# A recurrence of 2,048 steps on two engines: one product of the guarded norm issued behind the sum of squares

## The reference

```python
def step(h, inp):
    x_t, dt_t, B_t, C_t, xr_t = inp
    h_carrier = h.mean(axis=1)
    T = jnp.cos((c_phase(xr_t) - c_phase(h_carrier)) / 2.0) ** 2
    alpha = jnp.exp(dt_t[..., None] * A_neg)
    expo = 1.0 + (1.0 - alpha) * KAPPA * (1.0 - T[:, None, :])
    mag, ph = (c_mag(h), c_phase(h))
    cmag = jnp.minimum(jnp.exp(expo * jnp.log(mag + 1e-08)), 10.0)
    h = from_polar(cmag, ph)
    Bx = B_t[:, None, :, :] * (dt_t * x_t)[:, :, None, None]
    h = h + Bx
    h = from_polar(jnp.tanh(c_mag(h)), c_phase(h))
    y_t = jnp.einsum('bnc,bdnc->bd', C_t, h)
    return (h, y_t)
```

## Time and profile before

| | |
|---|---|
| median of 3 runs | 12692.01 us (12689.93 to 12693.14) |
| the profiled execution | 12694.92 us, span 12693.1 us |
| the recurrence's stretch in it | about 275 to 9440 us: 2,048 steps |
| busy in the whole span | PE 84%, DVE 80%, ACT 66%, PEld 42% |

### The profile page before, as it was taken

One profiled execution on the slowest core, in us unless ns is written; L12 is line 12 of the kernel. 1 busy time (PEld: TensorE's weight loads), 2 busy tenths in 40 slices (PEclk: granted clock), 3 DMA queues, 4 the chain that ended last, 5 costly groups with the idle time before them and its releaser, 6 DMA issues. The chain is left out here.

```text
span 12693.1 us, 256258 instructions
## 1 busy us (share of the span) xinstructions
PE 10620.3 (84%) x68398; PEld 5374.3 (42%) x68414; DVE 10121.4 (80%) x56587; ACT 8430.5 (66%) x42451; POOL 95.0 (1%) x165
## 2 busy tenths in 40 slices
PE   6888888888888888888888888888887978898998
PEld 5333333333333333333333333333344546653335
DVE  5888888888888888888888888888874948868875
ACT  6777777777777777777777777777764722264666
POOL 0000000000000000000000000000000100000000
PEclk8666667666666666666666666666678978998999
DMA  1000100001000100001000010001000000011100
GB/s 57 15 15 15 21 15 15 15 17 20 15 15 15 21 15 15 15 15 22 15 15 15 16 21 15 15 15 21 15 10 12 1 24 6 7 35 46 29 24 22
DMA packets 339618, 229.88 MB, mean 18 GB/s; under 512 B 27662, under 2 KB 324183, under 8 KB 337884
## 3 DMA queue, kind: packets, MB, share of 16 engines
q1 hardware_dynamic: 338140, 213.30, 7.9%
HBM read 187.41 MB, written 25.43 MB: 17 GB/s over the span
## 5 line engine op out<-in xcount | busy, mean ns | idle before, releaser
L548 PE MATMUL scan_p_car<-scan_warm 128*128 128x448 bf16 x15872 | 5455.5, 490 | 993.3 <-DVE scan_state_ps L674 985.4
L548 PEld LDWEIGHTS scan_p_car<-scan_warm 128*128 128x128 bf16 x15872 | 1513.7, 117 | 3681.5 <-DVE scan_state_ps L674 2094.0
L595 ACT ACTIVATE scan_act_ps<-scan_state_ps 128x64 f32<-128x64 f32 x2048 | 426.0, 208 | 1888.6 <-DVE scan_state_ps L674 1888.6
L595 ACT ACTIVATE scan_act_ps<-scan_act_ps 128x64 f32<-128x64 f32 (+1 forms) x8193 | 1611.6, 197 | 65.5
L536 PEld LDWEIGHTS scan_p_car<-scan_hs,scan_mean_mat 32*32 32x32 f32 x16392 | 372.2, 125 | 1846.5 <-DVE scan_hb L677 1834.2
L677 DVE SCALAR_TENSOR_TENSOR scan_uw<-scan_w,scan_rsq 128x64 f32<-128x64 f32 x2048 | 461.3, 225 | 854.2 <-ACT scan_rsq L595 854.2
L541 PE MATMUL scan_p_car<-scan_eps_row,ones 1*128 1x3 f32 x4102 | 1021.3, 316 | 39.1 <-DMA scan_a_log<-L_attn_a_A_log 38.9
L536 PE MATMUL scan_p_car<-scan_hs,scan_mean_mat 32*32 32x2 f32 x16392 | 548.5, 191 | 590.3 <-DVE scan_hb L677 568.0
L570 PE MATMUL scan_p_y<-scan_c_masked,scan_hb 128*64 128x4 f32 x16384 | 1037.8, 229 | 0.0
L674 DVE TENSOR_TENSOR scan_c<-scan_V,scan_power_ps 128x64 f32<-128x64 f32 x4096 | 724.6, 218 | 277.8 <-issue 47.6
L541 PEld LDWEIGHTS scan_p_car<-scan_eps_row,ones 1*128 1x128 f32 x4102 | 843.3, 255 | 72.0 <-DMA scan_a_log<-L_attn_a_A_log 39.3
(11 more groups left out here) (453 smaller groups left out, 18358.4 us busy)
## 6 DMA issues: line engine op xcount, KB each, us to landing
scan_step_in<-scan_scratch SPq DMA_DIRECT2D x520, 256.0 KB, 6.2
qk_scratch<-qkv_parts SPq DMA_DIRECT2D x32, 384.0 KB, 2.5
attn_qT<-qk_scratch SPq DMA_DIRECT2D x192, 64.0 KB, 2.2
attn_kT<-qk_scratch SPq DMA_DIRECT2D x192, 64.0 KB, 2.2
scan_scratch<-prep_dts SPq DMA_DIRECT2D x32, 256.0 KB, 2.1
x<-L_attn_a_x SPq DMA_DIRECT2D x1, 4096.0 KB
out<-x SPq DMA_DIRECT2D x1, 4096.0 KB
filter_in_taps<-c_kT SPq DMA_DIRECT2D x1, 2048.0 KB
```

The lines of the kernel that those rows point to most:

```text
L548: nc.tensor.matmul(p_car[slot][:, 64:512], warm[:, 0:P], warm[:, 64:512], start=True, stop=True)
L595: nc.scalar.activation(dst, src, func, **kw).then_inc(counts[par]["act"], 1)
```

## The change

The product `na` and the sum `r2` change places on VectorE. `na` no longer waits by itself for `sq0`, since `r2` in front of it has waited for `sq1`. The list `DVE_STEP` follows, so that the waits for `r2` (ScalarE's `l`, TensorE's matmuls) and for `na` (`n2`) count to the new places. No instruction is added or removed.

```diff
-DVE_STEP = ["c0", "c1", "w0", "w1", "sq0", "sq1", "na", "r2", "n2", "bx0", "bx1", "uw0", "uw1", "h0", "h1", "nh", "hp", "Vm", "dot", "dl", "s", "V"]
+DVE_STEP = ["c0", "c1", "w0", "w1", "sq0", "sq1", "r2", "na", "n2", "bx0", "bx1", "uw0", "uw1", "h0", "h1", "nh", "hp", "Vm", "dot", "dl", "s", "V"]
...
                                 tt(sem, sq[:, comp, :], w[:, comp, :], w[:, comp, :], ALU.mult)
-                            after(dve, "dve", "sq0", par, k)
-                            stt(sem, na[:, :], w[:, 0, :], 2 * EPS_PHASE, sq[:, 0, :], ALU.mult, ALU.add)
                             after(dve, "dve", "sq1", par, k)
                             tt(sem, r2[:, :], sq[:, 0, :], sq[:, 1, :], ALU.add)
+                            stt(sem, na[:, :], w[:, 0, :], 2 * EPS_PHASE, sq[:, 0, :], ALU.mult, ALU.add)
                             after(dve, "dve", "na", par, k)
                             tt(sem, n2[:, :], na[:, :], sq[:, 1, :], ALU.add)
```

## The result

The changed kernel took 12,744.3 us in the median of six executions, against 12,691.0 us for the kernel before in the same comparison: a ratio of 1.0038, 95% interval 1.0028 to 1.0049, so 36 to 62 us slower. One of the six was slow, 18,728.7 us at a mean granted clock of 0.555, and is left out of the ratio; the other five lie between 12,732.9 and 12,748.0 us. The forecast was 12,721 us and a slowdown. Its range (12,696 to 12,760) holds the measured time, which lies 1 us above the band of its main case (12,708 to 12,743); its 29 us are somewhat more than half of the 48 us that the ratio gives.

The account below looks back on a forecast made before the run. A dependency chain through `sq`, `r2`, `l`, `M`, `E`, `L1`, `R` bounds the kernel, no engine being full. 8 ns for late `ln2` plus 6 of extras, 14 ns a step, 29 us, gave a median of 12,721 us, range 12,696 to 12,760.

Parts of the forecast that it names:

- main case: Whole recurrence: 8 to 25 ns a step slower, 12,708 to 12,743 us; chance 0.60.
- `r2` starts at 388: VectorE, ns from the start of `sq0`: `r2` starts at 388 instead of 406, 18 earlier.
- the longer: Rival, own-result hand-over on VectorE of 52 ns: `r2` gains nothing, 44 ns a step lost, 12,782 us; chance 0.14.
- the shorter: Rival, own-result hand-over on VectorE below 30 ns: at 21 ns a gain of 18 ns a step, 12,655 us; chance 0.10.
- `na` takes the next slot, `n2` starts at 775: VectorE, ns from `sq0`: `na` starts at 523, ends at 741; `n2` starts at 775, 233 later than before.
- `ln2` is held by `n2`, `E` by `ln2`: ScalarE: `ln2` waits for `n2` until 1,035 instead of 1,027; `E`, queued behind it, also comes 8 ns later.
- The extras, 6 ns out of 0 to 17: Longer instructions from a standstill: 0 to 7 ns each for `r2` and `n2`, 0 to 3 for `ln2`; 6 taken.
- What is hidden: `bx0`, `bx1` move 0.24 us later inside VectorE's wait for `rsq`, 0.43 us in a plain step; TensorE's matmuls shift.
- The rule that the slots alone count: Rival from the Trainium skill, own-engine waits on VectorE cost nothing: 135 ns a step gained, 276 us, 12,416 us; chance 0.01.
- What the profile would show: Step time line: `r2` 0.39 and `n2` 0.78 behind `sq0`, `ln2` 0.03 behind `n2`; waits naming `n2`, a few tens of us.

## Why the prediction was right, and where its size was off

1. *`r2` starts at 388.* The time line has 0.38 to 0.39, the mean of the steps is 388, and the idle time in front of it is 34.1 ns, the hand-over that was taken from other layers. Right, and with it both rivals that hung on another hand-over, the longer and the shorter, are gone.
2. *`na` takes the next slot, `n2` starts at 775.* It starts 783 ns behind the first square on the mean, after another 34.1 ns of waiting. Right to 8 ns, and these belong to point 4.
3. *`ln2` is held by `n2`, `E` by `ln2`.* Right, and shown from four sides: free `n2` and the loss turns into a gain; one slot later costs nothing, two cost 44 ns; put `E` in front and it starts 0.24 behind `M`.
4. *The extras, 6 ns out of 0 to 17.* This is the term that was mis-sized. `na` follows `r2`, which starts from a standstill, by 142 ns and not by the slot of 135, so `n2` comes 7 ns later; and `n2` takes 233 ns and not 226, 7 more. `r2` takes 233 and not 227 as well, but `ln2` waits for `n2` and not for `M`, so this is hidden. The stretch agrees: 22.8 ns a step were measured where 8 were due without extras. So the extras are about 15 ns, near the upper end. The rows gave that end (`uw0` 225 against `na` 218) and I discounted it, because it was of another kind of instruction. 8 to 25 ns was the forecast's own range; 22.8 lies in it. Without extras the change would have cost 16 us, less than the 25 us that the prediction took for no change. So that the slowdown came out clear hung on the term that was put too small, and to that extent the call of "slower" was lucky; the mechanism was not.
5. *What is hidden.* `bx0`, `bx1` and the output product stayed hidden: VectorE still waits 0.21 us for `rsq`, as said. On TensorE the prediction gave no number, only that "the chain meets TensorE again only when `h1` is there". That holds for this change, which starts the three matmuls earlier: the mean starts 54 ns behind `h1` as before. But the cover is thin: the same matmuls 0.14 us later cost 65 us.
6. *The rule that the slots alone count.* By it the change would have gained 276 us. It is refuted for these instructions by the same 34.1 ns of idle time and by the measured slowdown.
7. *What the profile would show.* I had expected the waits to name `n2` as ScalarE's releaser. They don't: its group (which holds `lnh` too) has no idle time in front of it, because `M` is still running (6082.61 + 0.21) when `ln2` starts at 6082.77:

```profile
L595 ACT ACTIVATE scan_act_ps<-scan_norm_ps 128x64 f32<-128x64 f32 x4036 | 855.6, 212 | 0.0
```

An instruction that is late by less than the overlap leaves no trace in the waits. Only the distances from start to start show it.

## What to carry to other kernels

Where two short results leave one engine and the next engine takes them in a fixed order, what counts is which of the two has less to spare, not which the chain runs through today. Before moving a producer, compare its delay with its consumer's slack: here 241 ns of delay (233 predicted) and a sum that took 7 ns longer stood against 225 of slack, and a gain of 18 in front of them came to nothing. Put something independent between a short instruction and the one that reads it; where that can't be done, count, for instructions of this size, the hand-over (34 ns) and the standstill (7 ns) at each such place.

## What the runs showed of the hardware

- VectorE starts 128x64 instructions every 135 ns. One that reads the result of the one before starts 34 ns behind its end, for 128x64 as for 128x1536; for 128x64 that is 252 ns from start to start (`na` to `n2`).
- A sum that starts from a standstill takes 233 ns, the same sum in its slot 227, and the next instruction starts 142 ns behind it and not 135.
- A logarithm on ScalarE takes 208 ns from PSUM and 228 from SBUF; a sum on VectorE takes 233 ns into PSUM and 225 into SBUF, both from a standstill.
- One of eight constant matmuls a step taken away lowered TensorE's mean clock in the recurrence from 0.68 to 0.58 in one pair of kernels and from 0.70 to 0.61 in another.
- From the mean's first load on TensorE to `nsq` it takes 307 ns in steps at 1.00 and some 350 at 0.50: that is what the lower clock costs this step.
- The written-out steps hold pauses at fixed places, some 38 to 51 us in all in the kernels here; what makes them is open.
